# Moving the transposition of half of the next expert's rows from the fifth to the sixth unit of a fused attention and mixture-of-experts kernel

## The reference

```
def expert_step(acc, inp):
    gu, dp, w = inp
    gate, up = jnp.split(x @ gu.T, 2, axis=-1)
    hidden = jax.nn.silu(gate) * up
    y = hidden @ dp.T
    return (acc + w[:, None] * y, None)
out, _ = jax.lax.scan(expert_step, jnp.zeros_like(x), (gate_up_proj, down_proj, combine_w.T))
return out.reshape(b, s, h)
```

## Time and profile before

| what | value |
|---|---|
| median of 3 runs | 451.83 us (450.56 to 452.75) |
| profiled execution, its time | 451.6 us |
| its span, first to last instruction | 449.8 us |
| mean granted TensorE clock | 0.990 of full |
| busy: PE / DVE / ACT / POOL | 437.4 / 349.5 / 256.1 / 98.3 us |
| expert part, from about 169 to 441 us | PE busy throughout |

### The profile page before, as it was taken

One profiled execution on the slowest core, in us unless ns is written; L12 is line 12 of the kernel. 1 busy time (PEld: TensorE's weight loads), 2 busy tenths in 40 slices (PEclk: granted clock), 3 DMA queues, 4 the chain that ended last, 5 costly groups with the idle time before them and its releaser, 6 DMA issues.

```text
span 449.8 us, 7028 instructions
## 1 busy us (share of the span) xinstructions
PE 437.4 (97%) x2432; PEld 371.1 (83%) x2432; DVE 349.5 (78%) x663; ACT 256.1 (57%) x434; POOL 98.3 (22%) x130
## 2 busy tenths in 40 slices
PE   8999899999999999999999999999999999999992
PEld 6978788888887788888888888888888888888881
DVE  5866656755747668998898998988988888898852
ACT  4576535634546556657657566566666656657520
POOL 6071071271437351003003003003003003002111
PEclk9999999999999989999999999999999999999997
DMA  7997985324594476757757856856855856845311
GB/s 263 352 319 251 279 192 152 151 91 140 195 205 171 133 261 209 301 191 215 244 196 194 254 203 185 260 182 203 268 158 199 278 166 211 252 185 189 70 47 52
DMA packets 27775, 90.74 MB, mean 202 GB/s; under 512 B 2656, under 2 KB 8800, under 8 KB 27744
## 3 DMA queue, kind: packets, MB, share of 16 engines
q1 hardware_dynamic: 24288, 81.96, 56.4%
q0 software_dynamic: 3456, 8.40, 7.8%
HBM read 75.91 MB, written 14.45 MB: 201 GB/s over the span
## 4 chain that ended last, share of the span: by engine, by line
PE 96%; DVE 1%; ACT 1%; POOL 1%; issue 0%; POOLq 0%; DVEq 0%
PE PJ L464 13%; PE T L464 13%; PE PJ L465 7%; PE T L465 7%; PE SC L565 3%; PE T L278 3%; PE SC L566 3%; PE SC L567 3%; PE PJ L265 3%; PE PJ L267 3%; PE PJ L266 3%; PE SC L311 3%; PE R L565 2%; PE R L566 2%; PE R L567 2%; PE SC L265 2%
## 5 line engine op out<-in xcount | busy, mean ns | idle before, releaser
L991 DVE TENSOR_TENSOR ul<-ng,uh 128x1536 fp32r<-128x1536 f32 x64 | 112.5, 1758 | 1.0
L719 ACT ACTIVATE uh<-ng 128x1536 fp32r<-128x1536 f32 x64 | 94.8, 1481 | 0.0
L464 PE MATMUL PJ<-eb,uh 128*128 128x512 f32 x248 | 88.7, 398 | 0.0
L464 PE MATMUL T<-eb,uh 128*128 128x512 f32 x248 | 88.6, 397 | 0.0
L465 PE MATMUL PJ<-eb,ul 128*128 128x256 f32 x248 | 69.7, 281 | 0.0
L465 PE MATMUL T<-eb,ul 128*128 128x256 f32 x248 | 69.6, 281 | 0.0
L1494 POOL DMA_INDIRECT out<-ys,yidx x14 | 24.8, 1772 | 175.8 <-ACT ys L914 173.7
L464 PEld LDWEIGHTS PJ<-eb,uh 128*128 128x128 f32 x248 | 46.6, 188 | 11.2
L464 PEld LDWEIGHTS T<-eb,uh 128*128 128x128 f32 x248 | 46.6, 188 | 11.1
L465 PEld LDWEIGHTS T<-eb,ul 128*128 128x128 f32 x248 | 46.9, 189 | 1.3
L465 PEld LDWEIGHTS PJ<-eb,ul 128*128 128x128 f32 x248 | 46.8, 189 | 1.3
(11 more groups left out here) (251 smaller groups left out, 929.8 us busy)
## 6 DMA issues: line engine op xcount, KB each, us to landing
ng<-in_units SPq DMA_DIRECT2D x64, 768.0 KB, 4.3
vs<-in_ctxn SPq DMA_DIRECT2D x8, 768.0 KB, 5.5
kTs<-in_ctxT SPq DMA_DIRECT2D x8, 750.0 KB, 7.1
slots<-zero SPq DMA_DIRECT2D x8, 514.0 KB, 13.5
xe<-slots SPq DMA_DIRECT2D x8, 514.0 KB, 4.4
wTs<-in_weights SPq DMA_DIRECT2D x8, 512.0 KB, 8.3
xt<-in_x SPq DMA_DIRECT2D x7, 256.0 KB, 14.1
out<-xt SPq DMA_DIRECT2D x7, 256.0 KB, 4.4
```

The source lines that it names most:

```text
L464: nc.tensor.matmul(o[:, :].rearrange("p (h s) -> p h s", h=2), wh, both[:, k, :, :], start=k == 0, stop=False)
L719: nc.scalar.activation(o, i, ACT.Copy).then_inc(s, 1)
L991: v.tensor_tensor(o, whole, hi.bitcast(F32), ALU.subtract).then_inc(s, 1)
```

## The change

The half t = 0 is turned in unit i = 5 instead of i = 4, on PE, ACT and DVE alike. The half t = 1 stays in unit 6. The other expressions are rewritten so that they give the same numbers for t, for the counts waited for and for the banks.

```
-                if (i == 4 or i == 6) and (more or e == 0):
+                if (i == 5 or i == 6) and (more or e == 0):
-                    t = i // 6
+                    t = i - 5
                     nxt = 2 * it + e + 1
                     if t == 0:
                         pe.wait_ge(xe_in[(e + 1) % 2], 16 * (it + e + 1))
                     pe.wait_ge(e_lo, 2 * nxt + t)
...
-                    if (i == 4 or i == 6) and (more or e == 0):
-                        hi_e(2 * (2 * it + e + 1) + 1 + i // 6, (e + 1) % 2, i // 6, YB[(e + 1) % 2][i // 6])
+                    if (i == 5 or i == 6) and (more or e == 0):
+                        hi_e(2 * (2 * it + e + 1) + i - 4, (e + 1) % 2, i - 5, YB[(e + 1) % 2][i - 5])
...
-                    if (i == 4 or i == 6) and (more or e == 0):
-                        lo_e(2 * (2 * it + e + 1) + 1 + i // 6, (e + 1) % 2, i // 6, YB[(e + 1) % 2][i // 6])
+                    if (i == 5 or i == 6) and (more or e == 0):
+                        lo_e(2 * (2 * it + e + 1) + i - 4, (e + 1) % 2, i - 5, YB[(e + 1) % 2][i - 5])
```

## The result

The changed kernel took 455.77 us in the median (455.02 to 456.56, 4 runs), the kernel before 451.32 us beside it (450.56 to 452.75, 4 runs): a ratio of 1.0103, 95% interval 1.0076 to 1.0131. Timed again later, beside the last experiments, it took 454.80 us against 451.40, a ratio of 1.0089 (1.0050 to 1.0128). The forecast was 455.7 us, range 452.3 to 457.8.

What follows compares the result with a forecast made beforehand. The prediction took PE to bound the kernel, with no slack in the expert part. Waits of 2.72 us plus starts of 1.3 made 4.0 us on the profiled 451.6; with the median 0.23 us higher, it said 455.7 us, range 452.3 to 457.8.

Steps and rivals of the forecast that it cites:

- PE is the bound and has no slack in the expert part: Expert part, 169 to 441 us: PE busy all 272.00 us, so only matmuls removed or PE waits added move the end.
- Moved work costs nothing: Seven transpositions of 0.45 us move from behind unit 4's products to behind unit 5's on PE: sum 0.
- The wait of half 1 decides: Behind unit 6's products PE waits 0.38 us for half 0's split; P is unit 5's products' end; all waits 2.72 us.
- The first handover: Expert 0 to 1, DVE still behind: split ends at 193.67, PE ready at 193.18, a wait of 0.49 us.
- Starting again: PE's restart behind each of seven waits loses the weight load's overlap: 0.18 us each, 1.3 us, between 0 and 3.3.
- Sum: Whole kernel: waits 2.72 plus starts 1.3 make 4.0 us, giving 455.7 us, 0.9% slower.
- Nobody gets short by the delay: Work queued behind half 1's wait: ACT and DVE only gain slack, so the wait is neither repeated nor paid back.
- The met wait: Rival at each half 1: the split is visible before unit 6's products end, price 0, time 451.6 us; chance 0.25.
- The clock: Rival: each of seven waits on PE brings the half clock, 16 us more in all, 467.6 us; chance 0.03.
- What would show it: New PE entry, half 1's transposition released by DVE's split: 7 times, 0.4 to 0.6 us each, 3 to 4 total.

Runs made afterwards that it cites:

- free_after: Changed kernel, but half 1's transposition on PE asks only for the splits of the expert before: 451.14 us against 451.30, ratio 0.9989.
- both5: Kernel before, with both halves turned in unit 5 behind one wait, and both split at the end of unit 5's list: 451.31 us against 451.40, ratio 0.9989.
- split_first: Changed kernel, but DVE does the splits before the gate sum of the next unit: 452.65 us against 451.40, ratio 1.0037.
- free_before: Kernel before, with half 1's transposition asking only for the splits of the expert before: 451.03 us against 451.30, ratio 0.9976.

## Why the prediction was right, step by step

- **PE is the bound and has no slack in the expert part.** Right: 3.5 us of waits and starts lengthened the part by as much, and in each experiment its length moved with PE's waits.
- **Moved work costs nothing.** Nearly right: with everything moved and the wait gone (free_after) the ratio was 0.9989, but the expert part was 0.26 us longer. Where on PE these lie is not traced.
- **The wait of half 1 decides; split at P + 4.99, PE at P + 4.61.** Right in place, number and size. The split came at P + 4.99; PE was ready at P + 4.65, because the products by which I measured were unit 5's, 2.77 us long at that handover (220.69 to 223.46), and those ahead of half 1's transposition are unit 6's, 2.82. So the split was 0.34 us late at six handovers where I had 0.37.
- **The first handover, 0.49 us late.** Right in sign, too small: it was 195.48 - 194.78 = 0.70 us, at the edge of the 0.7 that I had named as a sign of a longer run of DVE. The run was longer. DVE in the changed kernel:

```profile
190.84 0.41 DVE L1306 TENSOR_TENSOR us<-T,us 128x256 f32<-128x256 f32 x1
191.48 0.43 DVE L1308 TENSOR_TENSOR hf<-us,hs 128x256 f32<-128x256 f32 x1 [0.22 <-ACT hs L932]
...
194.80 0.68 DVE L991 TENSOR_TENSOR eb<-R,eb 128x512 fp32r<-128x512 f32 x1
```

  From `us` to the end of the split it is 195.48 - 190.84 = 4.64 us, and I had taken 4.37 over unchanged. DVE was behind there, its gate sum came late, Silu on ACT after it, and `hf` had to wait 0.22 us for ACT.
- **Starting again, 0.18 us each.** The mis-sized term. That the weight load loses its cover is right; the loads (PEld) of the kernel before and of the changed one, each at half 1's transposition of the second handover:

```profile
227.56 0.48 PEld L278 LDWEIGHTS SC<-ident,xe 128*128 128x128 f32 x4
```

```profile
230.52 0.42 PEld L278 LDWEIGHTS SC<-ident,xe 128*128 128x128 f32 x4 [0.55 <-DVE eb L991]
```

  Before, the first load began 0.12 us ahead of its matmul (227.68), under the matmul before it; behind the wait load and matmul are recorded as starting together at 230.52. But the price is smaller than I took it: 0.05 us from the split's end to PE's start and 0.06 us in the matmuls that follow, 0.11 us, 0.8 us in all and not 1.3. The row at 49 us showed a start of wide matmuls with loads of 0.19 us; here narrow ones with loads of 0.14 us start, four in a row. The estimate by the Trainium skill ("TensorE: Matmul & The Clock Gate", section "LDWEIGHTS (loading the stationary operand)"), 107 ns for a bare load and 0.7 us for seven, came nearer in size; but only 0.06 of the 0.11 us lie in the pipe, the rest is the time until PE starts.
- **Sum.** 4.0 us forecast; 2.74 + 0.8 = 3.5 us in the waits and starts, 3.80 in the whole part. The starts were taken too high by 0.5 us, the first handover too low by 0.2 and the moved work by 0.3; these cancelled, so that the sum is closer than its terms. That the measured 455.77 us lies within 0.1 us of the forecast is luck: the kernel before measured 451.32 beside it and not 451.83, and timed again the changed kernel took 454.80.
- **Nobody gets short by the delay.** Right: at the second handover of the changed kernel DVE had 0.28 us of idle time right behind the split, and in the expert part no other new wait of PE appeared.
- **The rivals.** The met wait did not come about; the distance of a tenth of a unit between records of two engines was real. The clock stayed at full level through the expert part (1.00 in its window), with seven waits of up to 0.8 us in it.
- **What would show it.** The entry and its count were right. Its size was misjudged: 0.2 to 0.6 us in the brackets and 2.0 us in total where I wrote 0.4 to 0.6 and 3 to 4. The reason is the drawn end of the matmul ahead of a wait; from start to start the loss is there in full.

## What to carry to other kernels

When a step is moved, look for the waits that name it as well as for those that it contains: here a counter that only orders the two halves tied half 1 to half 0's split, and closing the distance from two units to one left it 0.34 us short on the engine that has no slack. The size can be read beforehand from the kernel as it is: the distance from the producer's end to the consumer's next place, each counted from one common event. If such a wait guards nothing, as here where the halves use different banks, loosening it costs nothing and makes the order free (both5 and free_after are level with the kernel before). But PE was full already, and no order tried here won time.

## What the runs showed of the hardware beyond that

- A matmul's drawn duration hides part of a wait behind it: 0.39 us lost from start to start were shown as 0.23, and 0.06 us (split_first) as nothing.
- A release that arrives just when PE is ready (split_first) still costs it 0.12 us: 0.06 to the start and 0.06 in the first matmuls. One that came 3.8 us early cost nothing (free_before).
- The half clock of PE ahead of the expert part lasted 3.4 us in seven of the ten profiled executions and 6.8 in two (the changed kernel's first profile and both5), and did not appear in one (split_first); there the first matmul of expert 0 came at 164.06 us, against 165.2 to 165.8 at 3.4 us and 167.1 to 167.4 at 6.8.
